# Second score tiles and v tiles alternate on TensorE, and image 1 takes the next statistics later

## What is computed

```python
h = _gn(x)                      # 32 groups of 8 channels, mean and variance over the image
q = h @ Wq + bq; k = h @ Wk + bk; v = h @ Wv + bv
scores = einsum('bnc,bmc->bnm', q, k) * scale
out = einsum('bnm,bmc->bnc', softmax(scores, axis=-1), v) @ Wo + bo
return x + out
```

## Time and profile before

| | us |
|---|---|
| median of 3 runs | 1807.21 (1807.15 to 1807.3) |
| profiled execution | 1807.02 |
| its span, first to last instruction | 1805.3 |
| TensorE busy | 1796.1 |
| VectorE busy | 1627.7 |
| ScalarE busy | 1070.1 |

### The profile page before, as it was taken

The page is one execution under the profiler, slowest core; times in us unless marked ns, Lnnn a source line. Parts: engine busy times, 40 slices in busy tenths (PEclk is TensorE's granted clock), DMA queues, the critical chain, the costliest instruction groups (busy, mean ns, idle before and its releaser), DMA issues.

```text
span 1805.3 us, 32859 instructions
## 1 busy us (share of the span) xinstructions
PE 1796.1 (99%) x11589; PEld 1641.9 (91%) x11589; DVE 1627.7 (90%) x2860; ACT 1070.1 (59%) x1417; POOL 104.8 (6%) x106
## 2 busy tenths in 40 slices
PE   9999999999999999999999999999999999999999
PEld 8989989999899998999998989989999899999989
DVE  7998999989998998999899998999999998998987
ACT  5565565665655656656566566565565655656653
POOL 0000000000000000000000000000000000000000
PEclk9999999999999999999999999999999999999999
DMA  3222132331213312222212232022321222211201
GB/s 117 59 71 61 21 70 58 70 70 22 59 58 70 70 38 44 66 61 70 57 25 70 58 70 65 16 70 58 70 70 32 49 60 68 70 46 35 70 12 36
DMA packets 28809, 101.92 MB, mean 56 GB/s; under 512 B 3189, under 2 KB 3962, under 8 KB 28794
## 3 DMA queue, kind: packets, MB, share of 16 engines
q0 software_dynamic: 9072, 33.03, 12.0%
q1 hardware_dynamic: 19722, 68.69, 11.7%
HBM read 68.16 MB, written 66.58 MB: 75 GB/s over the span
## 4 chain that ended last, share of the span: by engine, by line
PE 95%; DVE 3%; ACT 1%; issue 0%; DMA 0%; SPq 0%; DVEq 0%; ACTq 0%
PE ps_s L862 46%; PE ps_o L956 13%; PE ps_o L957 13%; PE ps_o L958 13%; PE ps_o L862 9%; DVE top L592 1%; ACT p_hi L356 0%; ACT s_buf L362 0%; DVE s_buf L622 0%; DMA s_buf<-in_L_conv_Wq_dram 0%; DVE p_lo L630 0%; ACT s_buf L348 0%; DVE o_buf L642 0%; DVE query_max L609 0%; DVE top_turned L597 0%
## 5 line engine op out<-in xcount | busy, mean ns | idle before, releaser
L956 PE MATMUL ps_o<-v_rows,p_hi 128*128 128x258 f32 x2048 | 577.7, 282 | 0.6 <-DVE v_lo L578 0.6
L958 PE MATMUL ps_o<-v_rows,p_lo 128*128 128x258 f32 x2048 | 576.1, 281 | 0.0
L957 PE MATMUL ps_o<-v_lo,p_hi 128*128 128x256 f32 x2048 | 575.4, 281 | 0.0
L356 ACT ACTIVATE p_hi<-s_buf 128x1024 fp32r<-128x1024 f32 x256 | 270.0, 1055 | 255.8 <-DVE s_buf L622 255.8
L348 ACT ACTIVATE s_buf<-ps_s 128x512 f32<-128x512 f32 x512 | 301.6, 598 | 196.1 <-PE ps_s L862 190.2
L862 PE MATMUL ps_s<-g_hi,h_hi 128*128 128x512 f32 x1024 | 399.2, 390 | 3.1 <-ACT s_buf L348 3.0
L862 PE MATMUL ps_s<-g_hi,h_lo 128*128 128x512 f32 x1024 | 398.6, 389 | 0.0
L862 PE MATMUL ps_s<-g_lo,h_hi 128*128 128x512 f32 x1024 | 398.5, 389 | 0.0
L956 PEld LDWEIGHTS ps_o<-v_rows,p_hi 128*128 128x128 f32 x2048 | 385.9, 188 | 2.1 <-issue 0.8
L957 PEld LDWEIGHTS ps_o<-v_lo,p_hi 128*128 128x128 f32 x2048 | 384.9, 188 | 1.5
L958 PEld LDWEIGHTS ps_o<-v_rows,p_lo 128*128 128x128 f32 x2048 | 384.5, 188 | 0.0
(11 more groups left out here) (95 smaller groups left out, 2211.5 us busy)
## 6 DMA issues: line engine op xcount, KB each, us to landing
x_t<-in_x_turned_dram SPq DMA_DIRECT2D x64, 512.0 KB, 4.0
out_dram<-in_x_dram SPq DMA_DIRECT2D x63, 512.0 KB, 7.1
out_dram<-o_buf POOLq DMA_DIRECT2D x63, 512.0 KB, 5.4
x_last<-in_x_dram SPq DMA_DIRECT2D x1, 512.0 KB, 7.6
out_dram<-o_buf SPq DMA_DIRECT2D x4, 128.0 KB, 1.9
s_buf<-in_L_conv_Wq_dram SPq DMA_DIRECT2D x1, 256.0 KB, 5.7
s_buf<-in_L_conv_Wk_dram SPq DMA_DIRECT2D x1, 256.0 KB, 5.9
s_buf<-in_L_conv_Wv_dram SPq DMA_DIRECT2D x1, 256.0 KB, 6.1
```

Of the source, the lines that this page charges most:

```text
L356: nc.scalar.activation(p_hi[c][:, rows, :], s_buf[c][:, rows, :], ACT.Exp, scale=SCALE).then_inc(p_hi_done, 1)
L956: nc.tensor.matmul(ps[:, 0:VC], p_hi[c][:, m, cols], v_hi[:, m, :], start=m == 0, stop=False)
L957: nc.tensor.matmul(ps[:, VC - C:VC], p_hi[c][:, m, cols], v_lo[:, m, :], start=False, stop=False)
L958: last = nc.tensor.matmul(ps[:, 0:VC], p_lo[c][:, m, cols], v_hi[:, m, :], start=False, stop=m == T - 1)
```

## The change

TensorE alternates: second score tile m of an image, then v tile m (`v_tile`), for m from 0 to 7, in images 0 to 30. The v tiles lie in the four banks `ps_o`, two in each, and no longer in `ps_g`; each bank waits for the finish that reads it. Second scores no longer wait for v_rests. Image 0's first attend goes by piece. ScalarE and VectorE take v_parts, v_rests, score copies and maxima in an order that follows this. In the loop, VectorE's `part_maxima(b, 1)` comes behind the last v_rest, and `difference(b, 1, 3)` behind the second g_rest. In image 1 (`late_stats`), the statistics of image 2 move from the first maxima to the second ones, and the two shifts on ScalarE behind the v_parts; GpSimd has image 1 written out for that.

```diff
@@ gpsimd: image 1 is written out, the loop starts at 2
             inverse_std(1)
             store(0, 0)
-            with pool.Fori(1, B - 1) as b:
+            store(0, 1)
+            inverse_std(2)
+            store(1, 0)
+            with pool.Fori(2, B - 1) as b:
                 inverse_std(b + 1)
...
@@ scalar
-            def v_part(b, i, nth=None):
-                act.wait_ge(v_ps, b * 4 + (i if nth is None else nth) + 1)
-                nc.scalar.activation(v_hi_chan[:, 2 * i:2 * i + 2, :], ps_g[i][:].rearrange("p (t n) -> p t n", t=2),
+            def v_part(b, i):
+                act.wait_ge(v_ps, b * 4 + (i + 1))
+                nc.scalar.activation(v_hi_chan[:, 2 * i:2 * i + 2, :], ps_o[i][:].rearrange("p (t n) -> p t n", t=2),
                                      ACT.Copy).then_inc(v_hi_done, 1)
...
                 for m in range(T):
                     scores_out(0, 0, m)
-                for nth, i in enumerate(FIRST_V):
-                    v_part(0, i, nth)
+                scores_out(0, 1, 0)
+                scores_out(0, 1, 1)
+                v_part(0, 0)
+                scores_out(0, 1, 2)
+                scores_out(0, 1, 3)
+                v_part(0, 1)
                 exponentials_hi(0, 0, 0)
-                scores_out(0, 1, 0)
                 exponentials(0, 0, 0)
-                scores_out(0, 1, 1)
+                scores_out(0, 1, 4)
                 exponentials_hi(0, 0, 1)
-                scores_out(0, 1, 2)
                 exponentials(0, 0, 1)
-                scores_out(0, 1, 3)
-                for i in (2, 3):
-                    exponentials_hi(0, 0, i)
-                    exponentials(0, 0, i)
-                for m in range(4, T):
-                    scores_out(0, 1, m)
+                scores_out(0, 1, 5)
+                v_part(0, 2)
+                exponentials_hi(0, 0, 2)
+                exponentials(0, 0, 2)
+                scores_out(0, 1, 6)
+                exponentials_hi(0, 0, 3)
+                scores_out(0, 1, 7)
+                v_part(0, 3)
+                exponentials(0, 0, 3)
...
-            def body(b):
-
-                shift(b + 1, 0)
-                shift(b + 1, 1)
+            def body(b, late_stats=False):
+
+                if not late_stats:
+                    shift(b + 1, 0)
+                    shift(b + 1, 1)
                 pair(b, 0, 0)
                 pair(b, 0, 1)
                 scores_out(b, 1, 0)
                 pair(b, 0, 2)
                 scores_out(b, 1, 1)
+                v_part(b, 0)
                 scores_out(b, 1, 2)
                 exponentials_hi(b, 0, 3)
+                exponentials(b, 0, 3)
                 scores_out(b, 1, 3)
-                exponentials(b, 0, 3)
-                for m in range(4, T):
-                    scores_out(b, 1, m)
-                for i in range(4):
-                    v_part(b, i)
+                v_part(b, 1)
+                scores_out(b, 1, 4)
+                scores_out(b, 1, 5)
+                v_part(b, 2)
+                scores_out(b, 1, 6)
+                scores_out(b, 1, 7)
+                v_part(b, 3)
+                if late_stats:
+                    shift(b + 1, 0)
+                    shift(b + 1, 1)
                 h_parts(b + 1)
...
@@ vector, first_image
                 difference(0, 0, 0)
-                v_rest(0, FIRST_V[0], 0)
                 difference(0, 0, 1)
-                v_rest(0, FIRST_V[1], 1)
+                v_rest(0, 0)
+                v_rest(0, 1)
                 p_rest(0, 0, 0)
                 difference(0, 0, 2)
                 difference(0, 0, 3)
                 p_rest(0, 0, 1)
-                v_rest(0, FIRST_V[2], 2)
-                v_rest(0, FIRST_V[3], 3)
+                v_rest(0, 2)
                 p_rest(0, 0, 2)
+                v_rest(0, 3)
                 p_rest(0, 0, 3)
...
-                scores_first(1)
+                for step in range(5):
+                    maxima(1, 0, step)
...
@@ vector, body(b, late_stats=False)
                 finish(b - 1, 1, 3)
-                for i in range(NP):
+                for i in range(NP - 1):
                     p_rest(b, 0, i)
-                for step in range(5):
-                    maxima(b, 1, step)
-                v_rest(b, 0)
+                if late_stats:
+                    channel_stats(b + 1)
+                p_rest(b, 0, NP - 1)
+                if late_stats:
+                    dve.wait_ge(bn_done, b * 4 + 8)
+                    channel_sums(b + 1)
+                    v_rest(b, 0)
+                    group_means(b + 1)
+                    group_spread(b + 1)
+                    v_rest(b, 1)
+                    group_variance(b + 1)
+                else:
+                    v_rest(b, 0)
+                    v_rest(b, 1)
+                maxima(b, 1, 0)
+                maxima(b, 1, 1)
+                if late_stats:
+                    turn_back(b + 1)
+                v_rest(b, 2)
+                maxima(b, 1, 2)
+                maxima(b, 1, 3)
+                maxima(b, 1, 4)
+                v_rest(b, 3)
                 part_maxima(b, 1)
-                for i in (1, 2, 3):
-                    v_rest(b, i)
                 query_maxima(b, 1)
...
                 difference(b, 1, 2)
-                difference(b, 1, 3)
                 finish(b, 0, 2)
                 finish(b, 0, 3)
                 g_rest(b + 1, 0)
                 g_rest(b + 1, 1)
+                difference(b, 1, 3)
                 p_rest(b, 1, 0)
...
@@ tensor
+            def v_tile(b, t):
+
+                if t % 2 == 0:
+                    after(pe, o_out, b * 8 + (t // 2 + 1 - 4))
+                product(ps_o[t // 2][:, (t % 2) * C:(t % 2 + 1) * C],
+                        [(h[:, kk, t * P:(t + 1) * P], w[:, kk, :]) for kk in range(K)
+                         for h, w in ((h_hi, vo_hi), (h_hi, vo_lo), (h_lo, vo_hi))],
+                        v_ps if t % 2 == 1 else None)
+
+            def scores(b, c, m):
...
-                if m in (2, 3) and first_v:
-                    pe.wait_ge(v_lo_done, FIRST_V.index(m) + 1)
-                elif m in (2, 3) and not ahead_of_v:
-                    pe.wait_ge(v_lo_done if c else g_lo_done, b * 4 + (m + 1))
+                if m in (2, 3) and c == 0:
+                    pe.wait_ge(g_lo_done, b * 4 + (m + 1))
...
                 if first:
-                    project_v(b, first=True)
-                    for m in range(T):
-                        scores(b, 1, m, first_v=True)
-                else:
-                    for m in range(T):
-                        scores(b, 1, m, True)
-                    project_v(b, 16)
+                    pe.wait_ge(out_bias_done, 1)
+                for m in range(T):
+                    scores(b, 1, m)
+                    v_tile(b, m)
                 for j in range(TQ):
-                    attend(b, 0, j, not first)
+                    attend(b, 0, j, True)
...
@@ tensor, last_image
-                project_v(b, 16)
+                for t in range(T):
+                    v_tile(b, t)
```

More of the change, by code:

```diff
@@ L486, in _ @@
             first_image()
-            body(1)
+            body(1, True)
             with act.Fori(2, B - 1) as b:
@@ L757, in scores_first, with body @@
                 maxima(b, 0, 4)
-            def body(b):
+            def body(b, late_stats=False):
                 part_maxima(b, 0)
-                turn_back(b + 1)
+                if not late_stats:
+                    turn_back(b + 1)
                 finish(b - 1, 1, 0)
```

31 lines of the change are left out of this document (8 added, 23 removed).

## The result

The changed kernel takes 1828.31 us (median of 4 runs, 1828.02 to 1828.49), the kernel before 1807.26 (4 runs, 1807.15 to 1807.57). The ratio is 1.0118, with a 95% interval of 1.0106 to 1.0130: slower by 21 us, where 1822.3 was forecast and 1828 was the upper end of the range.

The account below looks back on a forecast made before the run. TensorE was taken to bound the kernel, never waiting in the steady loop. Loop 15.3, image 0 2.0, image 1 -2.7 and start of image 2 0.5 sum to +15.1 on 1807.21: 1822.3 us, range 1815 to 1828.

Parts of the forecast that it names:

- The wait at score tile 3: First scores of images 2 to 31: TensorE waits for the fourth g_rest, 0.51 us an image, +15.3 us in all.
- The chain to it: Loop, behind the last v_rest: part_maxima 1.45 us later, ScalarE passes on 0.58, difference adds 1.13, fourth g_rest ends at 853.41.
- The step that failed: Loop's alternating stretch on TensorE: score and v tiles cost the same whichever comes between, so alternation adds nothing.
- Image 0: First attend waits 2.2 us for the last p_rest, the old v_rest wait goes: +2.0 us, bounds 0 and 2.5.
- Image 1: Score stall of 3.64 us goes, the first attend waits 1.7 + 0.1 us for the last v_rest: -2.7 us.
- The last image: Counted as zero, within 0.5 us: one wait for a score copy goes, one for a finish may come.
- the rival in which alternation costs: TensorE pays 0.01 us per change of tile kind, 15 changes in 31 images, 4.7 us, so 1827; chance 0.10.
- The room of 1.20 us ahead of score tile 3: Loop: VectorE's fourth g_rest can be up to 1.20 us later without loss; the two shifts take 1.71.

Follow-up runs that it names:

- b_both: Kernel before with part_maxima(b, 1) behind the last v_rest and difference(b, 1, 3) behind the second g_rest, without the alternation: 1822.43 us.
- a_d3_back: Changed kernel with difference(b, 1, 3) back ahead of the last finishes, the alternation kept: 1813.86 us.
- a_twos: The changed kernel with difference(b, 1, 3) back, and two score tiles then two v tiles at a time in images 1 to 30: 1810.19 us.
- a_fours: The changed kernel with difference(b, 1, 3) back, four score then four v tiles at a time, ScalarE's and VectorE's orders fitted: 1809.32 us.
- a_awake: Changed kernel with 17 matmuls whose results nobody reads filling the wait in image 0's first attend: 1828.46 us.
- b_d3: Kernel before with one edit, difference(b, 1, 3) behind the second g_rest: 1818.84 us.
- b_pm: Kernel before with one edit, part_maxima(b, 1) behind the last v_rest instead of the first: 1807.14 us.
- b_d3_rest: Kernel before with difference(b, 1, 3) behind the second g_rest, v_rests 0 to 2 ahead of part_maxima's transpose, its reduction behind v_rest 3: 1806.99 us.

## Why the prediction was wrong

The direction and the main mechanism were right. Point by point:

- **The wait at score tile 3.** Forecast 0.51 us an image, 0.50 in the profile, and b_both gives 15.4 for 15.3. The chain to it holds at each step: part_maxima 1.45 later, 0.58 of it passed on by ScalarE, the fourth g_rest late, and a restart of 0.13 (0.10 here at tile 3, some more at tile 2). The rule cited from the Trainium skill, "TensorE: Matmul & The Clock Gate", section "Architectural detail: the array is 16× 32×32, not 1× 128×128", that weight loads can be pulled ahead, doesn't hide this restart: 0.38 an image would be 11.4 in all, and b_both shows 15.4.
- **The step that failed** is "A score tile costs 1.36 us and a v tile 0.70 (5.61 us for eight) whichever comes between". A score tile behind a v tile costs 1.38. With 7 of them in 31 images, and a little for the changes back, that is 5.7 us, nearly all of the 6.0 between forecast and result; the other misses in the table nearly cancel (+1.5, +0.6, -0.8, -0.6 and -0.1 twice, together +0.5). It stood among the rivals with a chance of 0.10 and a price of 4.7. The argument there that stages "change kind too" and still make a busy image holds for a cost of 0.02 as well, since a slower pace is no wait. And the rival's "No row shows a score tile behind a v tile" is true of the rows that were read, but the trace of before has one such tile, in image 0, where the v tiles stand ahead of the second scores:

```profile
36.82 0.39 PE L862 MATMUL ps_s<-g_hi,h_hi 128*128 128x512 f32 x1
...
38.20 0.39 PE L862 MATMUL ps_s<-g_hi,h_hi 128*128 128x512 f32 x1
```

From 36.82 to 38.20 are 1.38 us. At 0.02 for each of 217 such tiles that is 4.3 us, and the forecast would have been 1826.6.

- **Image 0.** The wait was forecast at 2.2 and is 2.2. The half clock behind it, 1.5 us, was not. In the profiles of after, a_d3_back and a_twos it is there, in those of a_fours and a_awake it isn't. It isn't what put the result over the range: the two runs of after that read 1.000 took 1828.02 and 1828.24 us.
- **Image 1.** The stall of the second scores went, as forecast. The attend was to wait 1.8 and waits 0.97 (0.88 and a restart), which is 0.8 us better. VectorE's first difference and its last v_rest there:

```profile
88.54 2.36 DVE L637 TENSOR_TENSOR s_buf<-s_buf,row_max 128x1024 f32<-128x1024 f32 x2
...
109.06 0.68 DVE L593 TENSOR_TENSOR v_lo<-ps_o,v_rows 128x512 fp32r<-128x512 f32 x1
```

The work between them was estimated at 21.5 us and takes 21.2 (88.54 to 109.74). The larger part of the miss is where it starts: 1.65 us ahead of the stretch of 90.19, not 1.2. The last 0.2 come from the stretch itself, which is that much longer.

- **The last image.** It was counted as "zero, within 0.5" and is +0.6. Its v tiles wait for a finish, since they lie in the attend's banks:

```profile
1797.69 0.38 PE L897 MATMUL ps_o<-vo_hi,h_hi 128*128 128x256 f32 x1 [0.68 <-DVE o_buf L657]
```

- **The range** ended at 1828, 1 us above the rival in which alternation costs, and the result lies 0.3 over it. It took "some of the upper bound" only: with the prediction's own upper bounds for the loop (19.2) and image 0 (2.5), and that rival's 4.7, the sum is 1831.4. The one step whose row hadn't been read was priced at zero.
- **Room.** The room of 1.20 us ahead of score tile 3 is true, but b_d3 shows that VectorE has a second place with less, at v_rest 1. The change happens to move v_rests 0 and 1 forward, so the forecast of the kernel after did not depend on it, while the expectation for b_d3 failed by 11.6 us.

What stays open: what decides whether the half clock comes behind such a wait, and why a longer matmul runs a few per cent slower behind shorter ones.

## What to carry to other kernels

Where the bounding engine never waits, look for the room of every one of its waits before moving work on the engines that feed it; a shift of 1.1 us was free at one and cost 0.39 us an image at another. A new interleaving of two shapes of matmul has a price even without a wait, so price it by the number of changes, and look through the whole trace, the boundary images too, for one such change before pricing it at nothing. When a change has one part that gains in the boundary images and others that touch the loop, make the first alone: here it gives 3.2 us, and with the rest the kernel loses 21.

## What the runs showed of the hardware

- A score tile (six matmuls of 512 columns) behind a v tile (six of 256) takes 1.38 us in place of 1.36, and the stretch grows in proportion to the number of such changes (16.50, 16.52, 16.57, 16.68 us for 0, 1, 3, 7).
- A matmul that waited for a semaphore is followed late by the next one: 0.30 to 0.34 us behind in place of 0.23 with 512 columns (861.23 behind 860.93 and 862.95 behind 862.62), 0.19 to 0.22 in place of 0.12 with 256 (894.54 behind 894.35, 51.72 behind 51.50). The waits of 0.24 us in after and 0.30 in b_d3 don't show as idle time in the records.
- The granted clock fell to 0.50 for 3.4 us in 6 of these 13 profiles, each time behind a wait of TensorE of 2.2 to 2.7 us and while it was busy again: in image 0 in after, a_d3_back and a_twos, in image 1 in b_pm, b_both and b_d3_rest. Before, b_d3 and a_fours have the same waits and stayed at 1.00 in their profiles. Of 29 runs of the four kernels with no such wait, or with the wait filled, none reads 0.999.
